# A graph network of four layers on one core: an empty half group left out of two passes, sums copied later on ScalarE, and 20 of the record scatters moved into pair building

## The reference, cut to what matters

```python
# layer 0: mean over the neighbours, then a linear map
mean = segment_sum(h[src], dst) / maximum(count, 1)
out0 = concat([h, mean]) @ W.T + b
# layer 1: two relational convolutions, 8 relations over 4 bases (relu after the first)
m = sum_b comp[etype, b] * (h @ basis[b])[src] * edge_weight
out1 = segment_sum(m, dst) + bias + h @ loop_w
# layer 2: tensor product messages; w1..w4 come out of an MLP 8 -> 64 -> 64 -> 64 -> 512 with silu
s0, s1 = x0[src], x1[src]                     # 128 scalars and 128 vectors of 3
msg = [w1*s0*y0, w4*dot(s1, y1)], [w2*s0*y1, w3*s1*y0]
out2 = linear(segment_sum(msg, dst))          # 1024 summed values per node
# layer 3: an MLP on every edge, then one on every node
e = mish(mish(concat([h[src], h[dst], attr64]) @ W1 + b1) @ W2 + b2)
u = mish(concat([h, segment_sum(e, dst)]) @ W3 + b3) @ W4 + b4
out3 = layernorm(h + u) * gamma + beta
```

## Time and profile before

| | |
|---|---|
| time, median of 3 runs (range) | 2186.97 us (2186.95 to 2189.45) |
| the profiled execution's own time, and its span | 2186.25 us, 2184.4 us |
| busy in the span: PE, PEld, DVE, ACT, POOL | 1949.1 (89%), 1128.8 (52%), 1578.0 (72%), 1274.8 (58%), 1464.0 (67%) us |
| ordering, 62 to 187 us of the span | PE 106.5, DVE 115.9, ACT 82.3, POOL 99.2 us busy |
| pair building, 187 to 382 us | PE 159.0, DVE 171.9, ACT 150.9, POOL 146.5 |
| layer 0, 382 to 445 us | PE 54.5, DVE 46.9, ACT 6.1, POOL 51.0 |
| first convolution, 460 to 604 us | PE 136.6, DVE 49.7, ACT 23.9, POOL 112.3 |
| message pass, 789 to 1294 us | PE 482.9, DVE 382.6, ACT 326.7, POOL 379.3 |
| edge pass, 1364 to 2129 us | PE 752.1, DVE 627.0, ACT 579.7, POOL 631.3 |

### The profile page before, as it was taken

The page is one execution under the profiler, slowest core; times in us unless marked ns, Lnnn a source line. Parts: engine busy times, 40 slices in busy tenths (PEclk is TensorE's granted clock), DMA queues, the critical chain, the costliest instruction groups (busy, mean ns, idle before and its releaser), DMA issues. The chain is left out here.

```text
span 2184.4 us, 35611 instructions
## 1 busy us (share of the span) xinstructions
PE 1949.1 (89%) x11507; PEld 1128.8 (52%) x11507; DVE 1578.0 (72%) x2251; ACT 1274.8 (58%) x2062; POOL 1464.0 (67%) x1120
## 2 busy tenths in 40 slices
PE   0797888879998859999999988899999999999997
PEld 0685777446555534444444444455555555555543
DVE  8998998733423457777777754588888888888875
ACT  1567777021122236666666642677877777777753
POOL 1787777867700047777777742588888888888842
PEclk9998999889999979999999999899999999999999
DMA  2411000232144234433333302332222222222200
GB/s 118 166 21 49 0 0 0 76 96 72 23 134 120 67 96 127 133 92 90 97 89 93 93 25 73 111 112 73 80 81 73 78 78 73 73 73 80 66 1 23
DMA packets 78495, 165.22 MB, mean 76 GB/s; under 512 B 15999, under 2 KB 41016, under 8 KB 77220
## 3 DMA queue, kind: packets, MB, share of 16 engines
q0 software_dynamic: 34560, 94.69, 15.9%
q1 hardware_dynamic: 43800, 68.78, 9.6%
HBM read 139.86 MB, written 23.39 MB: 75 GB/s over the span
## 5 line engine op out<-in xcount | busy, mean ns | idle before, releaser
L936 PE MATMUL e_two_ps<-w,e_first 128*128 128x512 bf16 x1344 | 400.9, 380 | 1.4 <-DVE e_lin L2093 1.2
L683 POOL DMA_INDIRECT sorted_records<-edge_record,slot_row x160 | 252.0, 1575 | 64.3 <-issue 54.9
L1704 ACT ACTIVATE u_msg<-u_t,slot_record 128x128 f32<-128x128 f32 x672 | 214.5, 395 | 71.4 <-DVE u_t L1769 71.4
L936 PE MATMUL e_two_ps<-w,e_first_low 128*128 128x512 bf16 x672 | 255.4, 380 | 0.0
L2390 POOL DMA_INDIRECT e_got<-src_table,e_idx x168 | 206.3, 1228 | 67.5 <-issue 35.7
L1884 POOL TENSOR_TENSOR e_first_low<-e_first 128x1024 bf16<-128x1024 f32 x84 | 232.2, 2764 | 20.5 <-DVE e_first L2086 16.1
L1617 POOL TENSOR_TENSOR total<-total,u_part 125x1024 f32 x84 | 198.0, 2357 | 65.5 <-ACT u_part L1712 55.4
L1891 POOL TENSOR_TENSOR e_msg_low<-e_act 128x1024 bf16<-128x1024 f32 x82 | 195.6, 2385 | 30.3 <-DVE e_act L2098 29.4
L936 PEld LDWEIGHTS e_two_ps<-w,e_first 128*128 128x128 bf16 x1344 | 128.1, 98 | 143.2 <-issue 3.0
L1607 POOL DMA_INDIRECT u_got<-up_table,u_idx x168 | 162.0, 964 | 59.8 <-POOL u_idx L1601 33.4
L1668 PE MATMUL u_sum_ps<-u_msg,u_hot 128*125 128x512 f32 x336 | 179.8, 617 | 14.8 <-ACT u_msg L1704 14.8
(11 more groups left out here) (380 smaller groups left out, 4723.0 us busy)
## 6 DMA issues: line engine op xcount, KB each, us to landing
conv_w<-in_L_gnn_basis_dram SPq DMA_DIRECT2D x8, 1024.0 KB
sorted_records<-pairs SPq DMA_DIRECT2D x5, 1344.0 KB, 10.4
later_w<-in_L_gnn_W_dram SPq DMA_DIRECT2D x6, 1024.0 KB
attr_parts<-h SPq DMA_DIRECT2D x21, 256.0 KB, 2.1
e_attrT<-attr_parts SPq DMA_DIRECT2D x42, 128.0 KB
e_dst_all<-dst_row SPq DMA_DIRECT2D x42, 125.0 KB
edge_record<-in_edge_floats_dram SPq DMA_DIRECT2D x1, 3125.0 KB
pairs<-in_edge_floats_dram SPq DMA_DIRECT2D x1, 3125.0 KB
```

What stands on the lines that cost most here:

```text
L683: pg.nc.gpsimd.indirect_dma_start(out=pg.sorted, out_offset=bass.IndirectOffsetOnAxis(ap=pg.slot_row[:, j:j + 1], axis=0), in_=pg.edge_rec ...
L936: last = nc.tensor.matmul(out, lhsT, rhs, start=(n == 0), stop=(n == len(pairs) - 1))
L1704: last = nc.scalar.activation(msg[:, k, at * MUL:(at + 1) * MUL], t12[:, k % 2, of], ACT.Copy, scale=pg.record[:, bass.ds(t, 1), Y + m])
```

## The change

- **Scatters.** Ordering issues 42 scatters (IN_ORDER) in place of 54. Pair building issues 20: POOL's loop is written out for its first 40 rounds of two items, with one scatter behind every second round; the remaining 19 rounds stay a loop. Layer 0 issues 4 and 14 as before, "n1" 4 in place of 8 (these four have late records, for which pair building waits already, with FIRST = 62 in place of 54), and the first convolution 76 in place of 80.
- **Message pass, order on ACT.** `take_sum` stands behind the vector paths of tile 1 (previous group's second half) and of tile 3 (this group's first half), ahead of the small MLP of that step. POOL's additions stand behind the gathers of tiles 1 and 3.
- **Message pass, the end.** The last group does two tiles on PE, ACT and DVE. The sums of the last two half groups with edges (81 and 82) are added to the total by DVE, straight from PSUM (`add_last`), with no copy by ACT and no addition by POOL.
- **Edge pass, the end.** The first layer of units 82 and 83 is computed for 256 slots in place of 512, in all its instructions (the same slice is put into the activations, `widen1` and `final1`, not shown). The second layer, the scatter and the addition of unit 83 go. The remainders of the last two units left, 81 and 82, are made by DVE. Behind the loop PE does own parts 0, 1 and 2, the scatter of unit 82 and own part 3.

```diff
@@ -30,6 +30,7 @@
+HALVES = NH
@@ -46,8 +47,9 @@
-FIRST = 54
-BESIDE = (58, 72)
+FIRST, IN_ORDER = 62, 42
+BESIDE = 66
+SOON = EARLY + 4
@@ -481,7 +483,7 @@
-            scatter_records(pg, range(0, FIRST))
+            scatter_records(pg, range(0, IN_ORDER))
@@ -751,18 +753,26 @@
         def _(pool):
-            with pool.Fori(0, NI // 2) as i:
+            def cells_of(g, h):
+                t = g * 2
+                pool.wait_ge(used, g + 1)
+                cells = pg.pair_cell[:, bass.ds(t, 2), :].rearrange("p t (a d) -> p t a d", a=1)
+                for to, of in ((high, pg.pair_high), (rest, pg.pair_rest)):
+                    n = of.shape[2]
+                    last = nc.gpsimd.tensor_tensor(to[:, h, :, :, :], cells.broadcast_to([P, 2, n, CELL]),
+                                                   of[:, bass.ds(t, 2), :].rearrange("p t (n a) -> p t n a", a=1)
+                                                   .broadcast_to([P, 2, n, CELL]), ALU.mult)
+                last.then_inc(cells_made, 1)
...
+            beside = FIRST - IN_ORDER
+            for i in range(2 * beside):
+                cells_of(2 * i, 0)
+                cells_of(2 * i + 1, 1)
+                if i % 2 == 1:
+                    scatter_records(pg, [IN_ORDER + i // 2])
+            with pool.Fori(2 * beside, NI // 2) as i:
...
-                    g = 2 * i + h
-                    t = g * 2
-                    pool.wait_ge(used, g + 1)
-                    cells = pg.pair_cell[:, bass.ds(t, 2), :].rearrange("p t (a d) -> p t a d", a=1)
-                    for to, of in ((high, pg.pair_high), (rest, pg.pair_rest)):
-                        n = of.shape[2]
-                        last = nc.gpsimd.tensor_tensor(to[:, h, :, :, :], cells.broadcast_to([P, 2, n, CELL]),
-                                                       of[:, bass.ds(t, 2), :].rearrange("p t (n a) -> p t n a", a=1)
-                                                       .broadcast_to([P, 2, n, CELL]), ALU.mult)
-                    last.then_inc(cells_made, 1)
+                    cells_of(2 * i + h, h)
@@ -1152,11 +1162,11 @@
-            scatter_records(pg, range(FIRST, BESIDE[0]))
+            scatter_records(pg, range(FIRST, BESIDE))
...
-            scatter_records(pg, range(*BESIDE))
+            scatter_records(pg, range(BESIDE, EARLY))
@@ -1312,7 +1322,7 @@
         def _(pool):
...
-                scatter_records(pg, range(EARLY, EARLY + FIRST))
+                scatter_records(pg, range(SOON, EARLY + FIRST))
@@ -1514,7 +1524,7 @@
-                  pool_work=lambda pool: scatter_records(pg, range(BESIDE[1], EARLY)))
+                  pool_work=lambda pool: scatter_records(pg, range(EARLY, SOON)))
@@ -1556,16 +1566,20 @@
...
         def upper(x):
...
+        def tiles_of(at):
...
+            return TG if at < LAST else (HALVES - 2 * LAST) * TH
@@ -1623,9 +1637,9 @@
-                    if k == 0 and at > 0:
+                    if k == 1 and 0 < at < LAST:
...
-                    if k == 2:
+                    if k == 3 and at < LAST:
@@ -1635,7 +1649,6 @@
-            add(NH - 1)
@@ -1672,8 +1685,9 @@
             def body(g, r, at):
...
-                for k in range(TG):
-                    if k < TG - 1:
+                tiles = tiles_of(at)
+                for k in range(tiles):
+                    if k < tiles - 1:
@@ -1712,20 +1726,19 @@
             def body(g, r, at):
-                for k in range(TG):
+                for k in range(tiles_of(at)):
...
+                    if k == 1 and 0 < at < LAST:
+                        take_sum(2 * g - 1)
+                    if k == 3:
+                        take_sum(2 * g)
...
-                    if k == 0 and at > 0:
-                        take_sum(2 * g - 1)
-                    if k == 2:
-                        take_sum(2 * g)
...
-            take_sum(NH - 1)
@@ -1793,6 +1806,15 @@
+            def add_last(n):
+                at = nc.vector.value_load(pg.block_of_half[0:1, n:n + 1], min_val=0, max_val=NB - 1)
+                dve.wait_ge(scattered, TH * (n + 1) + 2 * TG)
+                dve.wait_ge(added, 2 * LAST - 1)
+                if n >= 2 * LAST:
+                    dve.wait_ge(last_added, n - 2 * LAST + 1)
+                into = total[:, bass.ds(at, 1), :].rearrange("p a d -> p (a d)")
+                nc.vector.tensor_tensor(into, into, sum_ps[n % 2][0:BN, :], ALU.add).then_inc(last_added, 1)
@@ -1809,12 +1831,14 @@
+            for n in range(2 * LAST - 1, HALVES):
+                add_last(n)
...
 def edge_mlp_pass(pg, table_src, by_dst, w_attr, w_attr_rest, w2, later, gathers, total, pre_ps):
...
-    UNITS = 2 * NG
+    UNITS, SECONDS = 2 * NG, HALVES
@@ -1857,6 +1881,10 @@
+        def slots_of(n):
...
+            return SG if n < 2 * (HALVES // 2) else (HALVES % 2) * HG
@@ -1880,12 +1908,12 @@
             def low_of_first(n, r, u):
...
-                full = first[:, r % 2, 2 * u:2 * u + 2, :]
-                nc.gpsimd.tensor_tensor(first_low[:, r % 2, 2 * u:2 * u + 2, :], full, upper(full),
+                full = first[:, r % 2, 2 * u:2 * u + 2, 0:slots_of(n)]
+                nc.gpsimd.tensor_tensor(first_low[:, r % 2, 2 * u:2 * u + 2, 0:slots_of(n)], full, upper(full),
...
             def low_of_second(n, u):
-                if n >= UNITS - 2:
+                if n >= SECONDS - 2:
@@ -1923,23 +1951,24 @@
+                size = slots_of(n)
...
-                    ps = pre_ps[u][:, i, :]
+                    ps = pre_ps[u][:, i, 0:size]
...
-                        for half, at in enumerate(blocks):
+                        for half, at in enumerate(blocks[0:size // HG]):
...
-                    nc.tensor.matmul(ps, w_attr[:, cols], attrT[:, h, :], start=False, stop=False)
-                    nc.tensor.matmul(ps, w_attr_rest[:, cols], attrT[:, h, :], start=False, stop=False)
-                    for k in range(TG):
+                    nc.tensor.matmul(ps, w_attr[:, cols], attrT[:, h, 0:size], start=False, stop=False)
+                    nc.tensor.matmul(ps, w_attr_rest[:, cols], attrT[:, h, 0:size], start=False, stop=False)
+                    for k in range(size // P):
...
-                                                    pg.ident16[:, :], start=False, stop=(k == TG - 1 and part == 1))
+                                                    pg.ident16[:, :], start=False, stop=(k == size // P - 1 and part == 1))
@@ -1954,10 +1983,10 @@
             def scatter(n, g, r, u):
-                if n < UNITS - 2:
+                if n < SECONDS - 2:
...
-                    pe.wait_ge(last_low2, n + 3 - UNITS)
+                    pe.wait_ge(last_low2, n + 3 - SECONDS)
@@ -1972,10 +2001,12 @@
             def body(n, g, r, u, at):
-                second_layer(n, g, r, u, 0)
+                if n < SECONDS:
+                    second_layer(n, g, r, u, 0)
...
-                second_layer(n, g, r, u, 1)
+                if n < SECONDS:
+                    second_layer(n, g, r, u, 1)
@@ -1987,19 +2018,18 @@
-            own_part(0)
-            own_part(1)
-            scatter(UNITS - 2, NG - 1, (NG - 1) % RING, 0)
-            own_part(2)
-            scatter(UNITS - 1, NG - 1, (NG - 1) % RING, 1)
-            own_part(3)
+            for b in range(NB - 2):
+                own_part(b)
+            for n in range(UNITS - 2, SECONDS):
+                scatter(n, n // 2, n // 2 % RING, n % 2)
+            own_part(NB - 2)
...
 ...
@@ -2028,6 +2058,8 @@
             def body(n, g, r, u, at):
...
+                if n >= SECONDS:
+                    return
...
@@ -2113,8 +2147,9 @@
             def body(n, g, r, u, at):
...
-                last = at == NG - 1 and u == 1
-                widen2(n, u)
+                last = n + 1 >= SECONDS
+                if n < SECONDS:
+                    widen2(n, u)
@@ -2128,7 +2163,8 @@
-                final2(n, u)
+                if n < SECONDS:
+                    final2(n, u)
@@ -2147,7 +2183,7 @@
-            for n in range(UNITS - 3, UNITS):
+            for n in range(UNITS - 3, SECONDS):
```

More of the change, by code:

```diff
@@ L1558, in message_pass @@
         (parts_made, cleared, hot_ready, scattered, layer_made, layer_done, low_made,
-         tp_ready, t12_ready, turned_made, q_made, msg_dve, msg_act, summed, added) = (
+         tp_ready, t12_ready, turned_made, q_made, msg_dve, msg_act, summed, added, last_added) = (
             ctx.enter_context(nc.semaphore(f"u_{n}")) for n in (
                 "parts_made", "cleared", "hot_ready", "scattered", "layer_made",
-                "layer_done", "low_made", "tp_ready", "t12_ready", "turned_made", "q_made", "msg_dve", "msg_act", "summed", "added"))
+                "layer_done", "low_made", "tp_ready", "t12_ready", "turned_made", "q_made", "msg_dve", "msg_act", "summed", "added", "last_added"))
         attr_in = [ctx.enter_context(nc.semaphore(f"u_attr_in{h}")) for h in range(2)]
@@ L2001, in grow1 @@
                 act.wait_ge(mish1_ready, n - 1 + 2)
```

(16 more changed lines are left out.)

## The result

The changed kernel takes 2155.82 us as a median of 4 runs (2154.93 to 2158.71), beside 2188.05 for the kernel before on the same chip: 32.2 us less, a ratio of 0.9852 (0.9841 to 0.9864). Forecast was 2162. A second profile of the same kernel, taken with the experiments, has a span of 2152.1.

What follows compares the result with a forecast made beforehand. PE was taken to bound the message and edge passes, DVE to be tightest in pair building. The terms -6.1 + 9 - 14.0 - 7.0 - 6.2 = -24.3 us gave 2162 us, range 2150 to 2174.

Steps and rivals of the forecast that it cites:

- Boundaries: Ends of ordering, first normalization and first convolution: fewer scatters let the next stage start 1.3, 2.9 and 1.9 us sooner, 6.1 together.
- Message groups: Message pass: moving ScalarE's copy behind tile 3 takes 0.35 us off each of 40 groups, 14.0 us (bounds 8 and 16).
- End of the message pass: Last message group: two tiles fewer and a DVE addition from PSUM end it 7.0 us sooner (bounds 5.6 and 8).
- Pair building: Pair building: 20 added scatters make four items take 6.94 us against 6.44; 10.0 us, taken as 9 us slower.
- The waits of this chain are in it whatever the order: Pair building: the POOL-PE chain of 6.94 us per round already includes its waits; written-out code may shorten its 1.61 a little.
- Edge pass: End of edge pass: 8.7 us of PE work go, a 2.5 us wait comes back; gain 6.2 us (bounds 5 and 8.7).
- PE waits 1.21 + 1.21 + 0.1: End of edge pass: PE waits 2.5 us before unit 81's product for DVE's last activation step and remainder.
- Boundary behind the message pass: Behind the message pass nothing starts for 6.1 us; the forecast kept this gap as it is, no gain.
- the boundaries move: Rival: the 6.1 us gap behind the message pass falls away or appears elsewhere, time 2156 or 2168; chance 0.10.
- The exchange on ScalarE: Rival, message pass: moving the copies buys nothing because POOL or DVE sets the pace, time 2176; chance 0.12.
- The scatters in the pair loop: Rival, pair building: scatters are hidden as POOL recovers delays in its waits, 1.4 us instead of 9, time 2155; chance 0.12.
- Long scatters: Rival, pair building: scatters lasting up to 4.47 us lose 75 us in the loop, time 2229; chance 0.05.

Runs made afterwards that it cites:

- rolled: The kernel before with POOL's pair-building loop left a loop and one repeated scatter in each of its first 20 four-item rounds: 2206.30 us, ratio 1.0074.

## Why the prediction was right, and where its sizes were off

The time lies in the range, and every term had its sign right. The chains named for the message pass and for pair building were right; the wait in the edge pass was worked out wrongly, and a term of 7.4 us was put at nothing. That 2162 came so near is in part luck: these errors have opposite signs. Point by point, against 24.3 us in all:

- **Boundaries (6.1 forecast).** 1.6, 2.9 and 1.95, together 6.5. At the end of ordering 1.6 is near the 1.3 forecast by luck. In all seven profiles with 54 scatters there the next stage starts 3.93 to 3.96 us behind POOL's last scatter, not 2.45, while it is 2.94 to 4.99 behind VectorE's end; and with POOL long done it starts 1.56 to 1.59 behind VectorE, not 0.39. At the other two ends the working held. Four scatters fewer at two stage ends is enough to let VectorE's end rule there.
- **Message groups (14.0).** 11.65 - 11.29 = 0.36 a group over some 41 groups is 14.8; two groups took 12.3 and 11.6, which takes back 1.3.
- **End of the message pass (7.0).** From tile 1's product, begun at 1272.42, to 1275.75 is 3.3 us, beside 10.03 before: 6.7. With the groups the pass lost 20.0 us of the 21.0 forecast.
- **Pair building (+9).** It cost 3.4 against the profile before, 3.4 to 4.6 against the five profiles with the old loop and no added scatter: a mis-sized term. "The waits of this chain are in it whatever the order" held: the chain is the one that I named. Its unit prices were too high: an item takes POOL 1.20 us and not 1.28 once a scatter makes it late, and PE's answer 1.44 and not 1.61 in written-out code, which `rolled` tells apart. I had allowed 1 us for the latter; it was 20 x 0.2 = 4.
- **Edge pass (6.2).** It gave 2.1 and 1.4 in the two profiles. The rest of what the stretch to the tail lost, 3.6 and 2.9, is the 1.8 of the output stage. The edge stage took 801.3 to 803.3 us in the six profiles with the old end and 800.7 to 802.0 in the five with the new one, so its gain is hardly more than the spread. The step that failed is "PE waits 1.21 + 1.21 + 0.1". I counted VectorE's two steps on unit 81, and not what is queued behind them ahead of the release: PE's scatter needs VectorE's addition of unit 79 too. The timeline of VectorE in the changed kernel has all four:

```profile
2079.22 1.23 DVE L2132 SCALAR_TENSOR_TENSOR e_act<-e_act,e_lin 128x1024 f32<-128x1024 f32 x1
2080.48 1.23 DVE L2138 TENSOR_TENSOR e_msg_low<-e_act 128x1024 bf16<-128x1024 f32 x1
2081.62 1.22 DVE L2113 SCALAR_TENSOR_TENSOR e_act<-e_act 128x1024 f32<-128x1024 f32 x1
2082.76 0.68 DVE L2146 TENSOR_TENSOR total<-total,e_sum_ps 125x512 f32 x1
...
2083.59 0.59 PE L1994 MATMUL e_sum_ps<-e_act,e_hot 128*128 128x512 bf16 x1 [4.80 <-DVE total L2146]
```

  From 2078.79, where PE falls idle, to 2083.44, where the addition ends, is 4.65 us, and 0.15 to PE's start. Behind it the own parts ran at a granted clock of 0.86.
- **Boundary behind the message pass (0).** It gave 5.6 us and 1.8 more in the output stage behind it. The step that failed is "I keep it as it is": the change itself lets POOL end earlier than the stage. I had the gap as a rival ("the boundaries move", 0.10), whose 2156 is nearer to what was measured than 2162, but put it down to pages of code, and the 6.09 us behind POOL's end did not move. The Trainium skill (Runtime: NRT & Kernel Launch, Instruction fetch mechanics) says that a taken branch to code outside the loaded pages stalls until the code is fetched. If that were the gap, it should move with the code in front; the runs show 6.08 to 6.10 behind POOL's end with POOL's loop rolled or written out. A fetch is not excluded. I could have asked from the earlier trace rows: POOL was the last engine there.

With the measured terms, 6.5 - 3.4 + 20.0 + 5.6 + 1.8 + 1.8 (edge pass) = 32.3 us, the difference of the medians is 32.2; terms from single profiles have a spread of a few us, so that they meet so well is chance. The forecast of 2162 had two errors against the kernel (pair building 5.6, boundary 7.4) and one in its favour (edge pass 4.4).

**The rivals.** The exchange on ScalarE did buy its 0.36 us a group. The scatters in the pair loop were neither hidden (0.07 us a round) nor at 0.50: 0.19. Long scatters did not come: 1.23 us each. By the lock that the Trainium skill describes (SBUF — State Buffer, SBUF: two separate sides) they should keep their short time beside VectorE's instructions with a PSUM operand, and the trace agrees.

## What to carry to other kernels

When work is put on an idle engine inside a loop that another one waits for, follow the chain through both engines and take its prices from rows in which that chain is late; rows in which the engine waits anyway have slack in them. At the end of a pass, list all that the releasing engine does between the last cover and the release, every queued instruction of other units too, and put independent work of the waiting engine (here two own parts, 6.6 us) in front of the wait. Ask at each stage end how far the next stage starts behind each engine's own end, in several profiles: the engine at which this distance is constant is the one that holds it. Let that engine end early, by giving its last instructions to another one. And count what the shorter wait gives back in the clock behind it (here 1.8 us on top of 5.6).

## What the runs showed of the hardware

- How far the next stage starts behind an engine's last instruction differs by stage as well as by engine. Behind VectorE's it was 0.32 to 0.33 us at two ends (six profiles) and 1.56 to 1.59 at the end of ordering. Behind POOL's last scatter it was 2.2 to 2.5 at two ends and 3.93 to 3.96 at the end of ordering (seven profiles). Behind POOL's last addition in the message pass it was 6.08 to 6.10 in all thirteen profiles, and at the end of pair building, behind a multiplication, 4.36 at most. The cause stays open.
- The same 16 matmuls took 3.56 us at a granted clock of 0.50 behind 9.66 us of idle time of PE, and 1.90 at 1.00 behind 1.83 us.
- The granted clock behind one and the same 2.6 us wait of PE was 1.00 in one execution and 0.67 over the next 5 us in another, and a stage of 160 us came out up to 6 us longer by it.
- A scatter between written-out multiplications held POOL for 1.23 us, in the chain for 0.2 us a round. None of the 20 in pair building lasted longer.
